# Local attention: places of the query transposition, of the key copy and of the second probability copy

## The reference

```
def _layer(x, wqkv, qs, ksc, wo, ...):
    h = shift_token(x)
    q, k, v = jnp.split(h @ wqkv, 3, axis=-1)      # 8 heads of 64
    q = l2norm(q) * qs
    k = l2norm(k) * ksc
    q, k = rotary_xpos(q, k)
    o = local_attention(q, k, v)                   # windows of 64, own and the one before, causal
    x = x + o @ wo
    ...                                            # gelu feed-forward
```

## Time and profile before

| | |
|---|---|
| median of 3 runs | 3042.26 us (3041.33 to 3042.64) |
| the profiled execution's own time | 3024.94 us |
| its span | 3023.0 us |
| mean granted TensorE clock | 0.959 of full |

### The profile page before, as it was taken

How to read it: one execution, slowest core, us unless ns; L and a number is a source line. 1 busy time by engine, 2 the same in 40 slices (tenths; PEclk the granted TensorE clock), 3 DMA queues, 4 the chain that set the end, 5 groups by cost and what they waited for, 6 DMA issues and landing times. The chain is left out here.

```text
span 3023.0 us, 67408 instructions
## 1 busy us (share of the span) xinstructions
PE 2741.2 (91%) x21388; PEld 1809.0 (60%) x21388; DVE 2122.7 (70%) x3740; ACT 1950.8 (65%) x5578; POOL 1046.4 (35%) x1228
## 2 busy tenths in 40 slices
PE   6799999997989789888789999998988999999898
PEld 3577897773654434435556666676435666666644
DVE  4566565666764679757678888886447888888767
ACT  4466565666753654353388888887437888888744
POOL 0233343330000544210055555554215555555431
PEclk9799998998999989889999999999999999999999
DMA  4200120000000000130000000000000000000000
GB/s 141 75 20 21 50 71 25 18 21 8 9 16 0 1 0 1 28 60 1 26 1 0 0 0 0 0 0 13 7 8 2 0 0 0 0 0 0 1 21 35
DMA packets 82996, 51.58 MB, mean 17 GB/s; under 512 B 28848, under 2 KB 75568, under 8 KB 82864
## 3 DMA queue, kind: packets, MB, share of 16 engines
q1 hardware_dynamic: 78768, 41.56, 4.9%
q0 software_dynamic: 4096, 8.40, 0.9%
HBM read 31.59 MB, written 18.35 MB: 17 GB/s over the span
## 5 line engine op out<-in xcount | busy, mean ns | idle before, releaser
L2147 ACT ACTIVATE probs<-banks,minus_max,rnorm 128x128 f32<-128x128 f32 x1024 | 460.1, 469 | 3.4 <-DVE minus_max L2243 3.4
L2018 PE MATMUL banks<-weights,hf 128*128 128x512 f32 x768 | 432.6, 647 | 24.8 <-POOL hf L462 13.5
L2061 POOL TENSOR_TENSOR qk_cross<-qk_raw,rope_scaled 128x512 f32<-128x512 f32 x256 | 325.5, 1272 | 34.5 <-DVE minus_max L2243 14.4
L2223 DVE COPY probs_t<-banks 128x512 f32<-128x512 f32 x256 | 176.2, 688 | 128.2 <-PE banks L1996 127.6
L2071 POOL TENSOR_TENSOR qk_rot<-qk_rot,rnorm 128x512 f32<-128x512 f32 x128 | 133.4, 1042 | 325.9 <-DVE qk_rot L2276 318.1
L2147 ACT ACTIVATION_READ_ACCUMULATOR probs<-banks,minus_max,rnorm 128x1 f32 x1024 | 222.7, 217 | 0.0
L834 ACT ACTIVATE probs<-banks,minus_max 128x128 f32<-128x128 f32 (+1 forms) x512 | 207.9, 425 | 14.3 <-DVE minus_max L873 12.2
L1996 PEld LDWEIGHTS banks<-ident,probs 128*128 128x128 f32 x1024 | 126.9, 141 | 135.2 <-issue 101.4
L2010 PE MATMUL banks<-v_tok,probs_t 128*64 128x64 f32 x3072 | 173.4, 228 | 22.7 <-DVE probs_t L2223 22.7
L2257 DVE TENSOR_REDUCE sumsq<-qk_sq 128x16 f32<-128x1024 f32 x128 | 154.8, 1209 | 26.9 <-issue 19.9
L2267 DVE TENSOR_TENSOR qk_rot<-qk_raw,rope_scaled 128x512 f32<-128x512 f32 x256 | 166.9, 693 | 5.7
(11 more groups left out here) (353 smaller groups left out, 7094.8 us busy)
## 6 DMA issues: line engine op xcount, KB each, us to landing
sorted_x<-zero_rows SPq DMA_DIRECT2D x10, 512.0 KB, 6.2
rows_in<-sorted_x SPq DMA_DIRECT2D x18, 256.0 KB, 3.0
sorted_y<-rows_out SPq DMA_DIRECT2D x18, 256.0 KB, 2.4
x_res<-in_x SPq DMA_DIRECT2D x8, 512.0 KB, 6.5
out_x<-x_res SPq DMA_DIRECT2D x16, 256.0 KB, 2.0
w1b<-in_L_ffn_w SPq DMA_DIRECT2D x8, 256.0 KB, 4.4
s_branch<-in_L_ffn_w SPq DMA_DIRECT2D x8, 256.0 KB, 6.4
w1g<-in_L_ffn_W SPq DMA_DIRECT2D x8, 256.0 KB, 3.0
```

Source lines behind the costliest of these rows:

```text
L2018: pe.matmul(ps[:, misc(k, j)], hf[:, n // 2 % 2, 0, n % 2 * P:(n % 2 + 1) * P], wqkv[:, w:w + QW], start=True, stop=True).then_inc(*S[name ...
L2061: return pool.tensor_tensor(by_half(tw[:, n, at]), by_half(qk[:, n, at])[:, :, ::-1, :], tab[:, n, 2 * w + 1].rearrange("p (a d) -> p a d" ...
L2147: last = act.activation(pr[:, k % 2, head], ps[:, 2 * (k % 2) + par, c * P:(c + 1) * P], ACT.Exp, scale=rn[:, k % 4, head:head + 1], bias= ...
L2223: dve.tensor_copy(pt[:, h], ps[:, 4]).then_inc(*S["turned_sb"].inc)
```

## The change

On TensorE the query transposition of k+1 moves from right behind the scores to behind the q projection, ahead of the first half of the probabilities' transposition. `MISC` follows: the addition's bank is now the first of the seven, the q projection the second, the query transposition the third. On ScalarE the copy of the transposed query moves from the head of the slot to behind the copy of q, and the copy of the transposed key moves ahead of the exponentials of heads 0 and 1. On VectorE the copy of the second half of the probabilities moves ahead of the straight products. Nothing is added or removed; GpSimd, SyncE and the DMAs are untouched.

```
--- before.py
+++ after.py
@@ -1896,8 +1896,8 @@
         S["loaded"].base += 16 * len(ahead)
 
 
-MISC = [("qt_sb", 1), ("added", -3), ("q_sb", 3), ("kt_sb", 1), ("k_sb", 3), ("v_sb", 1), ("ot_sb", -2)]
-QT_AT, OUT_AT, Q_AT, KT_AT, K_AT, V_AT, OT_AT = range(7)
+MISC = [("added", -3), ("q_sb", 3), ("qt_sb", 1), ("kt_sb", 1), ("k_sb", 3), ("v_sb", 1), ("ot_sb", -2)]
+OUT_AT, Q_AT, QT_AT, KT_AT, K_AT, V_AT, OT_AT = range(7)
 
 
 def local_weights(area, a, layer):
@@ -2104,8 +2104,6 @@
                 def slot(i, k):
                     if here(i, k):
                         pe_scores(pe, i, k)
-                    if here(i, k + 1):
-                        pe_turn_qk(pe, i, k, QT_AT, "qt")
                     if here(i, k - 3):
                         pe_free(pe, i, k, OUT_AT)
                         pe.wait_ge(*S["ot_sb"].at(i, k - 3))
@@ -2114,6 +2112,8 @@
                         mm.then_inc(*S["o_ps"].inc)
                     if here(i, k + 3):
                         pe_project(pe, i, k, k + 3, Q_AT, "q")
+                    if here(i, k + 1):
+                        pe_turn_qk(pe, i, k, QT_AT, "qt")
                     if here(i, k - 1):
                         pe_turn(pe, i, k - 1, 0)
                     if here(i, k + 1):
@@ -2150,11 +2150,6 @@
                     return last
 
                 def slot(i, k):
-                    if here(i, k + 1):
-                        act.wait_ge(*S["qt_ps"].at(i, k + 1))
-                        act.wait_ge(*S["scores"].at(i, k - 1))
-                        act.activation(qt[:, (k + 1) % 2], bank(ps, misc(k, QT_AT), 4, P), ACT.Copy)\
-                            .then_inc(*S["qt_sb"].inc)
                     if here(i, k + 2):
                         act.wait_ge(*S["k_sb"].at(i, k + 2))
                         act.wait_ge(*S["sumsq"].at(i, k + 1))
@@ -2165,16 +2160,21 @@
                         act.wait_ge(*S["straight"].at(i, k + 1))
                         act.wait_ge(*S["crossed"].at(i, k + 1))
                         act.activation(qk[:, (k + 3) % 2, 0:QW], ps[:, misc(k, Q_AT)], ACT.Copy).then_inc(*S["q_sb"].inc)
+                    if here(i, k + 1):
+                        act.wait_ge(*S["qt_ps"].at(i, k + 1))
+                        act.wait_ge(*S["scores"].at(i, k - 1))
+                        act.activation(qt[:, (k + 1) % 2], bank(ps, misc(k, QT_AT), 4, P), ACT.Copy)\
+                            .then_inc(*S["qt_sb"].inc)
+                    if here(i, k + 1):
+                        act.wait_ge(*S["kt_ps"].at(i, k + 1))
+                        act.wait_ge(*S["scores"].at(i, k - 1))
+                        act.activation(kt[:, (k + 1) // 2 % 2, :, (k + 1) % 2 * P:((k + 1) % 2 + 1) * P],
+                                       bank(ps, misc(k, KT_AT), 4, P), ACT.Copy).then_inc(*S["kt_sb"].inc)
                     if here(i, k):
                         act.wait_ge(*S["rowmax"].at(i, k))
                         act.wait_ge(*S["turned"].at(i, 2 * (k - 2)))
                         act.wait_ge(*S["rowsum"].at(i, k - 2))
                         exps(i, k, range(0, 2))
-                    if here(i, k + 1):
-                        act.wait_ge(*S["kt_ps"].at(i, k + 1))
-                        act.wait_ge(*S["scores"].at(i, k - 1))
-                        act.activation(kt[:, (k + 1) // 2 % 2, :, (k + 1) % 2 * P:((k + 1) % 2 + 1) * P],
-                                       bank(ps, misc(k, KT_AT), 4, P), ACT.Copy).then_inc(*S["kt_sb"].inc)
                     if here(i, k + 3):
                         act.wait_ge(*S["k_ps"].at(i, k + 3))
                         act.activation(qk[:, (k + 3) % 2, QW:], ps[:, misc(k, K_AT)], ACT.Copy).then_inc(*S["k_sb"].inc)
@@ -2257,6 +2257,8 @@
                         dve.tensor_reduce(ss[:], by_head(sq[:]), AX.X, ALU.add).then_inc(*S["sumsq"].inc)
                         dve.wait_ge(*S["sumsq"].at(i, k + 2))
                         dve.tensor_scalar(ss[:], ss[:], 1e-24, None, ALU.max).then_inc(*S["v1"].inc)
+                    if here(i, k - 1):
+                        turned(i, k - 1, 1)
                     if here(i, k + 2):
                         n = (k + 2) % 4
                         dve.wait_ge(*S["k_sb"].at(i, k + 2))
@@ -2267,8 +2269,6 @@
                             last = dve.tensor_tensor(by_head(st[:, n, at]), by_head(qk[:, n % 2, at]),
                                                      tab[:, n % 2, 2 * w:2 * w + 1].to_broadcast([P, HEADS, DH]), ALU.mult)
                         last.then_inc(*S["straight"].inc)
-                    if here(i, k - 1):
-                        turned(i, k - 1, 1)
                     if here(i, k + 2):
                         n = (k + 2) % 4
                         dve.wait_ge(*S["straight"].at(i, k + 2))
```

More of the change, by code:

```diff
@@ L2152, in slot @@
                 def slot(i, k):
[L2153 to L2157, removed]
                     if here(i, k + 2):
@@ L2172, in slot @@
                         exps(i, k, range(0, 2))
[L2173 to L2177, removed]
                     if here(i, k + 3):
```

## The result

| | kernel before | changed kernel |
|---|---|---|
| median | 3041.8 us (3037.75 to 3042.64) | 3074.18 us (3072.29 to 3076.71) |
| ratio to the kernel before | | 1.011, 95% interval 1.0092 to 1.0127 |
| span of the profiled execution | 3023.0 us | 3072.2 us |
| first to last row maxima (line 2239) | 1320.4 us (1527.2 to 2847.6) | 1358.6 us (1538.1 to 2896.7) |

The account below looks back on a forecast made before the run. Bound: a once-per-slot loop of waits between VectorE and TensorE. Idle +0.21, dependent sum +0.12, short instruction -0.03, scores wait -0.08 gave +0.22 us per slot; over 120 slots +26.4 us, 3068.7 us; range 3046 to 3090.

Parts of the forecast that it names:

- The new loop: VectorE's gap-free work to the addition, then TensorE's query transposition waiting for it, first-half transposition, first copy; every slot.
- the signs: What would show it right, including a new TensorE wait of 0.4 to 0.7 us ahead of the query transposition.
- The idle time: VectorE's idle from the addition's end to the first copy of probabilities: 1.24 us in place of 1.03.
- the high end: Idle time 1.30 us, with 0.49 for a transposition group behind other work; all high terms together 0.45 us per slot.
- the low end: Idle time 1.20 us from a release of 0.05 us; all low terms together 0.03 us per slot, +4 us.
- The dependent sum: On VectorE, the sum now directly follows the straight products it reads and waits for their end: +0.12 us per slot.
- Rival 1: On VectorE, the sum directly behind the products costs nothing extra: 3054.3 us; chance 0.12.
- The short instruction: On VectorE, the next start behind it, 0.26 or 0.20 us before, taken as 0.20: mean gain 0.03 us.
- Given back: VectorE's wait for the scores at the loop's edge goes: 0.08 us per slot.
- Rival 4: VectorE reaches the addition sooner, gap-free part under 7.55 us, so TensorE's 8.79 us bounds the slot: 3006; chance 0.12.
- Rival 2: TensorE's k projection waits for ScalarE's query copy, a further 0.15 us per slot: 3087 us; chance 0.08.
- Rival 3: TensorE's wait for the addition exists but costs what the old one did, terms cancelling: 3042 us; chance 0.08.

Follow-up runs that it names:

- e2: Changed kernel with VectorE's second copy of probabilities put back behind the straight products, leaving only the TensorE, ScalarE and bank orders; ratio 1.0106, 3070.03 us.
- e3: Changed kernel with the output projection moved behind the q projection in TensorE's order and in `MISC`; ratio 1.0017, 3044.28 us.
- e5: Changed kernel with VectorE's addition of the output projection moved ahead of the row maxima; ratio 0.9755, 2965.03 us.
- e6: Changed kernel with VectorE's reciprocal of the next tile's row sums moved between the straight products and their sum; ratio 1.006, 3058.7 us.
- e4: Changed kernel with GpSimd's two input copies in the loop cut to 8 and 7 columns, leaving some inputs stale; ratio 1.0072, 3060.63 us.
- e1: Kernel before with only VectorE's second copy of probabilities moved ahead of the straight products; ratio 0.9814, 2984.41 us.
- e11: e1 with VectorE's addition moved ahead of the row maxima, TensorE and ScalarE orders as in the kernel before; ratio 1.0005, 3020.89 us.
- e10: Changed kernel with GpSimd's wait for the row maxima placed ahead of both crossed products instead of between them; ratio 1.0139, 3063.46 us.

## Why the prediction was right

It was right in sign, in mechanism and within its range. Its size was 6 us short by the medians and 12 us by the stretch, and per slot it was +0.22 us against a measured +0.37, so that the time came out this close is in part luck. By its own steps:

- *The new loop.* The wait stands where it was put, in every slot, and e2, e3 and e5 show that it is the cause. TensorE's wait is 0.81 us, longer than the 0.4 to 0.7 us of the signs. **The idle time** was put at 0.81 + 0.43 = 1.24 us and is 1.34. The group of four behind the wait takes 0.49 (1750.80 to 1751.29) where 0.43 was taken; this stood in the working as the high end, 1.30. The other 0.04 lie between the release and the copy: 0.85 us without this group, in place of the 0.81 of the earlier trace rows. The release alone, 1750.67 to 1750.80, is 0.13 us and not the 0.05 of the low end.
- *The dependent sum.* 1755.96 - 1754.64 = 1.32 us against 1.21: 0.11, forecast 0.12. Rival 1, by which it costs nothing, falls by this row and by e6, where the reciprocal finds room between the two without moving the sum, and itself starts 0.08 us before the products' end (1761.29 against 1761.37). The prediction cites the Trainium skill for the rival, "VectorE: DVE Perf Modes", section "The DRAIN you can't avoid". That section says that the semaphore costs nothing extra, and also that a next instruction that is not held starts earlier. The second statement agrees with the reciprocal's row; the first differs from the 0.11 us, and the measurement decides.
- *The short instruction*, line 2259: the next one starts 1754.03 - 1753.87 = 0.16 us behind it, where 0.20 was taken. In the mean over 32 slots it was 0.23 before and is 0.17.
- *Given back*: the wait for the scores is gone, as forecast, and was worth more than the 0.08 of the earlier trace rows, which shows it in 9 of 33 slots only. From the scaled output's start to that of the row maxima there were 0.73 us before and there are 0.61 now, means over 32 slots: 0.13.
- **The term that was missing** is GpSimd. The prediction looked only at its multiplication of the keys and put it at nothing; with the straight products 0.6 us later, they and the sum now meet its input copies: (1.51 - 1.32) + (1.23 - 1.14) = 0.28 us in every second slot, 0.14 per slot. About 0.02 of it was there before. e4 gives 13.5 us for it by the medians.
- *The sum.* Idle 0.31, dependent sum 0.11, GpSimd 0.14, less 0.13 for the scores and less 0.06 for the short instruction: 0.37. The slot grew from 9.02 us (32 slots in 288.78 us; the prediction's 9.09, from 33 slots in 300, was too rough a count) to 9.39, so by 0.37. Over the 112 slots in the loops that is 41 us. The two attention stretches, first to last row maxima, grew by 20.9 us each, and the part between them shrank from 195.2 to 191.4 us, which makes the 38.2 us of the stretch; the medians say 28 to 39.
- *Rival 4* had TensorE's own work as 8.79 us per slot, 8.72 with the right count. e1 and e5 show 8.53 and 8.44: taking one wait off the slot did not leave the rest as it was. The gain that was there to be had was 53 us in e1 and 73 in e5, not 36. It came with VectorE's gap-free part no shorter (in e1 8.53 - 0.48 = 8.05 us, against the 7.89 of the prediction): what had to shrink was the chain outside it, and not, as the rival's condition said, that part.
- *Rival 2* did not happen: no wait of TensorE for the query copy is in the view of waits. *Rival 3* falls with 1.34.

## What to carry to other kernels

In a pipeline with banks shared by turns, a moved instruction inherits the wait of whoever had the bank before. Look up which engine reads that bank, whether that engine waits for what comes behind the moved instruction, and close the loop on paper: gap-free part on the one engine, plus release, plus all that the other must do before it releases back. If it binds, move the reader ahead of its engine's long work rather than undo the order: here that turned 1.1% slower into 2.5% faster (0.9755). Undoing the order gave 1.9% (e1), and in the old order the same early addition lost all of that (e11): where the reader can go depends on when its data is made.

## What the runs showed of the hardware that was not expected

**VectorE and GpSimd hold each other.** An instruction of VectorE with two SBUF operands that starts beside a GpSimd product or copy is not done before that is. minus_max took 0.17 us alone, 0.30 in the changed kernel and 0.69 in e6, and in e6 it ends 0.01 to 0.02 us behind the product. The straight products took 1.48 beside the input copies and 1.28 else; the second of them ends 0.55 us behind the first copy's end (1764.84 and 1765.39). e4 gave 13.5 us back by making these copies short. It works the other way too: GpSimd's copy on line 462 took 0.40 us in the kernel before and 0.77 beside the products. The step on line 2259, with one SBUF operand, was held as well: 0.44 us in e10 in place of 0.17, with its end at 1754.90, 0.03 us behind that of the copy on line 2090. The reductions and the copies out of PSUM, 1.21 to 1.23 and 0.69 us, showed no such change in any run. The Trainium skill has this rule, and it should have been weighed ahead: "SBUF — State Buffer", section "SBUF: two separate sides", says that a VectorE instruction with two SBUF inputs and a GpSimd instruction that reads SBUF take the shared ports one at a time, for the whole instruction. The rows above agree.

**A short instruction is not the time it takes.** In the loop, minus_max at 0.17 us or 0.30 us led to the same start of the next instruction, 0.29 us later, as the queue's own records ahead of that one reach to 0.24 us. So here a saving on minus_max shows only where it had taken more than 0.3 us.

**Open.** Why TensorE's own work per slot is about 0.09 us shorter in e5 than in e1 (8.44 against 8.53, by the starts of line 2257 over 16 slots from 1700 us) was not tried by itself. Its orders differ: three transpositions in a row in e5, matrix products on both sides of the query's in e1.
